# GpSimd's gathers wait for TensorE's counts; masks in the accumulating form with scaled scores; x in fours from tile 8; no dummy products

## What is computed

```
inputs = front_emb[movie_id]                 # 2048 x 64, gathered
true_w, true_b = after_emb[labels], after_bias[labels]
samp_w, samp_b = after_emb[sampled_ids], after_bias[sampled_ids]
true_logits    = sum(inputs * true_w) + true_b - log(expected_count(labels))
sampled_logits = inputs @ samp_w.T + samp_b - log(expected_count(sampled_ids))
sampled_logits = where(sampled_ids == label, sampled_logits - 1e9, sampled_logits)
loss = logsumexp([true_logits, sampled_logits]) - true_logits
```

## Time and profile before

| | before |
|---|---|
| median of 3 runs | 61.03 us (60.61 to 61.16) |
| the profiled execution | 60.93 us |
| its span | 59.0 us |
| GpSimd busy | 40.1 us (68%), 48 instructions |
| VectorE busy | 44.7 us (76%) |
| ScalarE busy | 42.1 us (71%) |
| TensorE busy | 33.5 us (57%) |
| bytes read from HBM | 2.13 MB |

### The profile page before, as it was taken

One profiled execution on the slowest core, in us unless ns is written; L12 is line 12 of the kernel. 1 busy time (PEld: TensorE's weight loads), 2 busy tenths in 40 slices (PEclk: granted clock), 3 DMA queues, 4 the chain that ended last, 5 costly groups with the idle time before them and its releaser, 6 DMA issues.

```text
span 59.0 us, 603 instructions
## 1 busy us (share of the span) xinstructions
PE 33.5 (57%) x137; PEld 22.3 (38%) x137; DVE 44.7 (76%) x129; ACT 42.1 (71%) x69; POOL 40.1 (68%) x48
## 2 busy tenths in 40 slices
PE   0000093998349295997995969696989594000000
PEld 0000044634125254873772556364745481000000
DVE  3799888859688828995897997994999994490830
ACT  5305996489958092999979979999999949209020
POOL 4076777767777777767777776777777677776000
PEclk9999999999999999999999999999999999998555
DMA  0472122212100111100111101010201101101100
GB/s 0 172 192 50 45 62 64 53 45 50 22 22 22 22 42 24 24 22 22 28 25 36 22 22 28 23 23 23 55 24 23 23 23 31 37 23 23 23 0 6
DMA packets 1715, 2.17 MB, mean 37 GB/s; under 512 B 944, under 2 KB 944, under 8 KB 1712
## 3 DMA queue, kind: packets, MB, share of 16 engines
q0 software_dynamic: 1280, 1.59, 11.9%
q1 hardware_dynamic: 432, 0.55, 3.3%
HBM read 2.13 MB, written 0.01 MB: 36 GB/s over the span
## 4 chain that ended last, share of the span: by engine, by line
POOL 63%; issue 21%; DMA 7%; POOLq 2%; DVE 2%; ACT 1%; DVEq 0%
POOL x_rows L221 27%; POOL t_rows L221 23%; POOL w_rows L221 13%; DMA t_rows<-after,rows 4%; DMA id_cols<-ids 3%; POOLq L57 2%; DVE prod L504 0%; ACT rest L371 0%; ACT ratio L369 0%; DVE rows L414 0%; DVE neg_gap L536 0%; DVE wrap L412 0%; DVE loss L539 0%; DVE wrapped L413 0%; DVEq L502 0%
## 5 line engine op out<-in xcount | busy, mean ns | idle before, releaser
L327 ACT ACTIVATE psum<-psum,lowest 128x1024 f32<-128x1024 f32 x16 | 17.2, 1074 | 4.0 <-DVE lowest L494 3.9
L494 DVE CUSTOM_DVE_ANT_0 psum<-psum,masks 128x1024 f32<-128x1024 f32 x16 | 19.5, 1233 | 0.7 <-PE psum L279 0.6
L221 POOL DMA_INDIRECT x_rows<-front,rows x16 | 16.2, 1013 | 4.9 <-issue 4.9
L221 POOL DMA_INDIRECT t_rows<-after,rows x16 | 15.3, 956 | 4.9 <-issue 4.9
L277 PE MATMUL psum<-wT_high,xT 128*128 128x512 f32 x32 | 13.7, 429 | 3.7 <-ACT psum L327 3.7
L279 PE MATMUL psum<-b_parts,ones 128*128 128x512 f32 x32 | 12.7, 396 | 0.0
L278 PE MATMUL psum<-wT_low,xT 128*128 128x512 f32 x32 | 12.6, 395 | 0.0
L308 ACT ACTIVATE masks<-sample_ids,neg_label 128x1024 f32<-128x1024 int32 x8 | 9.2, 1144 | 3.1 <-DMA sample_ids<-sample_row 3.1
L221 POOL DMA_INDIRECT w_rows<-after_twice,rows x8 | 7.7, 965 | 3.8 <-issue 2.1
L313 ACT ACTIVATE masks<-masks,ln_big 128x1024 f32<-128x1024 f32 x8 | 9.2, 1147 | 0.0
L277 PEld LDWEIGHTS psum<-wT_high,xT 128*128 128x128 f32 x32 | 6.0, 188 | 7.3 <-issue 6.5
(11 more groups left out here) (79 smaller groups left out, 30.4 us busy)
## 6 DMA issues: line engine op xcount, KB each, us to landing
sample_ids<-sample_row SPq DMA_DIRECT2D x1, 512.0 KB, 3.9
x_rows<-front,rows POOLq DMA_INDIRECT x16, 2.5
t_rows<-after,rows POOLq DMA_INDIRECT x16, 2.4
w_rows<-after_twice,rows POOLq DMA_INDIRECT x8, 2.5
id_cols<-ids SPq DMA_DIRECT2D x1, 20.0 KB, 1.6
out<-loss SPq DMA_DIRECT2D x1, 8.0 KB, 1.4
```

The lines of the kernel that those rows point to most:

```text
L221: return pool.indirect_dma_start(dst, None, table, bass.IndirectOffsetOnAxis(ap=rows[:, col:col + 1], axis=0))
L327: nc.scalar.activation(logits(t), logits(t), ACT.Exp, bias=lowest[:, t:t + 1], scale=-1.0, accum_out=sums[:, t:t + 1]).then_inc(exp_ok, 1)
L494: V.tensor_tensor_reduce(out=logits(t), in0=logits(t), in1=masks[:, t, :], scale=1.0, scalar=3e38, op0=ALU.add, op1=ALU.min, accum_out=low ...
```

## The change

- **GpSimd.** Twenty-one of the gathers get a wait in front of them, for counts that TensorE gives: transposes of w for w tile 6 and x tile 0, of the bias for x tile 2, of x for x tiles 4 and 5, and finished scores (logits_ok) for later x tiles and for the label tiles. The order of the gathers stays. The count for each tile stands in the two tuples SCORED_BEHIND_X and SCORED_BEHIND_LABELS.
- **Masks.** VectorE's masks are 1 where the ids match, else 0, made by a tensor_scalar that also writes out a sum (accum_out to hits, which nothing reads), from a float copy of the sample ids that ScalarE makes first. ScalarE's masks lose their factor of 1e9. The scores are made smaller by 2 to the power -30 (in the scaling of x and of the bias), and the reduction multiplies by 2 to the power 30 after it has added the mask.
- **x by fours.** Tiles 8 to 11 and 12 to 15 become groups of four: one turn, one raise and one lower each. All places of turning, raising, lowering and masking in the loop are written out anew. Two masks are made ahead of the loop instead of four.
- **Dots.** One over eight tiles behind tile 11, one over four behind tile 15, instead of three over four.
- **No dummy products.**

```diff
--- before.py
+++ after.py
@@ -15,19 +15,24 @@
 BATCH = 2048
 SAMPLE_TILES = SAMPLES // P
 TILES = BATCH // P
-NEG_INF = -1e9
 BANK = 512
 SLOTS = 3
 QUARTERS = 4
 CORR = SAMPLE_TILES + TILES
 
+SHRINK = 2.0 ** -30
+
 SPREAD = P * (CORR + TILES)
 
-X_GROUPS = [(0, 1), (1, 2)] + [(t, t + 2) for t in range(2, TILES, 2)]
+X_GROUPS = [(0, 1), (1, 2), (2, 4), (4, 6), (6, 8), (8, 12), (12, 16)]
 ACT_MASKS = (0, 1, 2, 5, 8, 10, 12, 14)
 
+SCORED_BEHIND_X = (0, 0, 0, 0, 0, 0, 1, 1, 1, 2, 2, 3, 4, 5, 5, 6)
+SCORED_BEHIND_LABELS = (7, 8, 8, 9, 10, 10, 11, 11, 12, 13, 13, 14, 14, 15, 16, 16)
+
 BATCHED = 12
-T_GROUPS = [(0, 4), (4, 8), (8, 12), (12, 13), (13, 14), (14, 15), (15, 16)]
+T_GROUPS = [(0, 8), (8, 12), (12, 13), (13, 14), (14, 15), (15, 16)]
+BATCHES = 2
 
 SQRT_HALF = 0.70710677
 LOG_P = (0.070376836, -0.1151461, 0.116769984)
@@ -74,7 +79,7 @@
         neg_label = sb("neg_label", [P, TILES])
         sample_ids = sb("sample_ids", [P, SAMPLES], i32)
         ident = sb("ident", [P, P])
-        ln_big = sb("ln_big", [P, 1])
+        sample_f = sb("sample_f", [P, SAMPLES])
 
         w_rows = sb("w_rows", [P, SAMPLE_TILES, TWICE + 1])
         x_rows = sb("x_rows", [P, TILES, AUG])
@@ -117,6 +122,7 @@
 
         lowest = sb("lowest", [P, TILES])
         sums = sb("sums", [P, TILES])
+        hits = sb("hits", [P, TILES])
         log_sums = sb("log_sums", [P, TILES])
         base = sb("base", [P, TILES])
         dots = sb("dots", [P, TILES])
@@ -146,7 +152,7 @@
             return slice(a * P, b * P)
 
         def group_of(t):
-            return t if t < 2 else t // 2 + 1
+            return t if t < 2 else t // 2 + 1 if t < 8 else t // 4 + 3
 
         def w_cols(q):
 
@@ -180,6 +186,7 @@
         x_high_ok = sem("x_high_ok")
         xT_ok = sem("xT_ok")
         logits_ok = sem("logits_ok")
+        sample_f_ok = sem("sample_f_ok")
         act_square = sem("act_square")
         act_mask = sem("act_mask")
         dve_mask = sem("dve_mask")
@@ -222,13 +229,26 @@
                                                bass.IndirectOffsetOnAxis(ap=rows[:, col:col + 1], axis=0))
 
             pool.wait_ge(rows_ok, 1)
+
             for j in range(SAMPLE_TILES):
+                if j == 6:
+                    pool.wait_ge(w_turned, 1)
                 gather(w_rows[:, j, :], after_twice, j).then_inc(w_in[j // 2], 16)
             for g in range(len(X_GROUPS)):
                 for t in range(*X_GROUPS[g]):
+                    if t == 0:
+                        pool.wait_ge(w_turned, 2)
+                    elif t == 2:
+                        pool.wait_ge(b_turned, 3)
+                    elif t in (4, 5):
+                        pool.wait_ge(x_turned, t - 3)
+                    elif t >= 6 and SCORED_BEHIND_X[t] > SCORED_BEHIND_X[t - 1]:
+                        pool.wait_ge(logits_ok, SCORED_BEHIND_X[t])
                     gather(x_rows[:, t, 0:EMBED], front, MOV + t).then_inc(x_in[g], 16)
             for k, (a, b) in enumerate(T_GROUPS):
                 for t in range(a, b):
+                    if t == 0 or SCORED_BEHIND_LABELS[t] > SCORED_BEHIND_LABELS[t - 1]:
+                        pool.wait_ge(logits_ok, SCORED_BEHIND_LABELS[t])
                     gather(t_rows[:, t, :], after, LAB + t).then_inc(t_in[k], 16)
 
         @block.tensor
@@ -258,11 +278,6 @@
                     m = nc.tensor.transpose(psum[0:EMBED, x_bank(g), i * P:(i + 1) * P], x_rows[:, t, 0:EMBED],
                                             ident[:, :])
                 m.then_inc(x_turned, 1)
-
-            def keep_busy(n):
-                for _ in range(n):
-                    nc.tensor.matmul(psum[:, 7, :], ones[:, :], ones[:, 0:1].to_broadcast([P, BANK]),
-                                     start=True, stop=True)
 
             def score(t):
                 if t >= SLOTS:
@@ -280,25 +295,22 @@
                 m.then_inc(logits_ok, 1)
 
             turn_w(0)
-            keep_busy(2)
             turn_w(1)
-            keep_busy(4)
             turn_w(2)
             turn_b(0)
             turn_b(1)
             turn_b(2)
-            keep_busy(3)
             turn_w(3)
             turn_x(0)
             turn_b(3)
             turn_x(1)
+
+            turned_behind = {1: 2, 2: 3, 4: 4, 6: 5, 9: 6}
             for t in range(TILES):
-                if t % 2 == 0 and 2 <= t < TILES - 2:
-                    turn_x(group_of(t + 2))
                 pe.wait_ge(xT_ok, group_of(t) + 1)
                 score(t)
-                if t == 0:
-                    turn_x(group_of(2))
+                if t in turned_behind:
+                    turn_x(turned_behind[t])
 
         @block.scalar
         def _(act):
@@ -310,8 +322,7 @@
 
             def hit(t):
                 act.wait_ge(act_square, ACT_MASKS.index(t) + 1)
-                nc.scalar.activation(masks[:, t, :], masks[:, t, :], ACT.Exp, bias=ln_big[:, 0:1],
-                                     scale=-256.0).then_inc(act_mask, 1)
+                nc.scalar.activation(masks[:, t, :], masks[:, t, :], ACT.Exp, scale=-256.0).then_inc(act_mask, 1)
 
             def raise_w(q):
                 act.wait_ge(w_turned, q + 1)
@@ -320,7 +331,7 @@
             def raise_x(g):
                 act.wait_ge(x_turned, g + 1)
                 n = x_cols(g).stop - x_cols(g).start
-                nc.scalar.mul(xT[0:EMBED, x_cols(g)], psum[0:EMBED, x_bank(g), 0:n], -1.0).then_inc(x_high_ok, 1)
+                nc.scalar.mul(xT[0:EMBED, x_cols(g)], psum[0:EMBED, x_bank(g), 0:n], -SHRINK).then_inc(x_high_ok, 1)
 
             def exps(t):
                 act.wait_ge(lowest_ok, t + 1)
@@ -328,6 +339,7 @@
                                      accum_out=sums[:, t:t + 1]).then_inc(exp_ok, 1)
 
             act.wait_ge(row_in, 16)
+            nc.scalar.copy(sample_f[:, :], sample_ids[:, :]).then_inc(sample_f_ok, 1)
             act.wait_ge(labels_ok, 1)
             square(0)
             hit(0)
@@ -343,12 +355,12 @@
             raise_w(2)
             hit(2)
             act.wait_ge(b_turned, 2)
-            nc.scalar.copy(b_parts[0:2, 0:BANK], psum[0:2, 4, :]).then_inc(b_low_ok, 1)
+            nc.scalar.mul(b_parts[0:2, 0:BANK], psum[0:2, 4, :], SHRINK).then_inc(b_low_ok, 1)
             square(5)
             raise_w(3)
             raise_x(0)
             act.wait_ge(b_turned, QUARTERS)
-            nc.scalar.copy(b_parts[0:2, BANK:], psum[0:2, 5, :]).then_inc(b_high_ok, 1)
+            nc.scalar.mul(b_parts[0:2, BANK:], psum[0:2, 5, :], SHRINK).then_inc(b_high_ok, 1)
             raise_x(1)
             hit(5)
             raise_x(2)
@@ -356,10 +368,11 @@
 
             between = {0: (square, 8), 1: (hit, 8), 3: (square, 10), 4: (hit, 10), 6: (square, 12), 7: (hit, 12),
                        9: (square, 14), 10: (hit, 14)}
+            raised_behind = {1: 3, 3: 4, 6: 5, 9: 6}
             for t in range(TILES):
                 exps(t)
-                if t % 2 == 0 and t + 4 < TILES:
-                    raise_x(group_of(t + 4))
+                if t in raised_behind:
+                    raise_x(raised_behind[t])
                 if t in between:
                     make, u = between[t]
                     make(u)
@@ -381,8 +394,8 @@
                 dve.wait_ge(step, linked[0])
 
             def make_mask(t):
-                V.tensor_scalar(masks[:, t, :], sample_ids[:, :], label[:, t:t + 1], -NEG_INF, ALU.is_equal,
-                                ALU.mult).then_inc(dve_mask, 1)
+                V.tensor_scalar(masks[:, t, :], sample_f[:, :], label[:, t:t + 1], None, ALU.is_equal, ALU.add,
+                                accum_out=hits[:, t:t + 1]).then_inc(dve_mask, 1)
 
             def lower_w(q):
                 dve.wait_ge(wT_high_ok, q + 1)
@@ -401,12 +414,11 @@
             def lower_x(g):
                 dve.wait_ge(x_high_ok, g + 1)
                 n = x_cols(g).stop - x_cols(g).start
-                V.scalar_tensor_tensor(xT[EMBED:, x_cols(g)], psum[0:EMBED, x_bank(g), 0:n], -1.0,
+                V.scalar_tensor_tensor(xT[EMBED:, x_cols(g)], psum[0:EMBED, x_bank(g), 0:n], -SHRINK,
                                        xT[0:EMBED, x_cols(g)].bitcast(f32), ALU.mult, ALU.subtract).then_inc(xT_ok, 1)
 
             V.memset(b_parts[:, :].bitcast(f32), 0.0)
             V.memset(ones[:, :].bitcast(f32), 1.0).then_inc(dve_consts_ok, 1)
-            V.memset(ln_big[:, :], math.log(-NEG_INF))
             dve.wait_ge(limits_ok, 1)
             dve.wait_ge(ids_in, 16)
             V.tensor_scalar(wrap[:, :], id_cols[:, :], 0.0, float(VOCAB), ALU.is_lt, ALU.mult)
@@ -470,20 +482,18 @@
             V.tensor_tensor(count[:, :], count[:, :], below[:, :], ALU.add).then_inc(count_ok, 1)
 
 
+            dve.wait_ge(sample_f_ok, 1)
+            make_mask(DVE_MASKS[0])
             lower_w(0)
             lower_w(1)
             dve.wait_ge(log_count_ok, 1)
             split_b(0, 3)
             lower_w(2)
-            dve.wait_ge(row_in, 16)
-            make_mask(DVE_MASKS[0])
```

(30 more changed lines are left out.)

## The result

| | before | changed |
|---|---|---|
| median, side by side on one chip | 61.09 us (60.61 to 61.34, 4 runs) | 64.69 us (64.50 to 65.66, 4 runs) |
| the profiled execution | 60.93 us | 64.5 us |
| its span | 59.0 us | 62.5 us |
| neg_gap starts at | 56.33 | 59.77 |

The changed kernel takes 1.060 times as long (95% interval 1.055 to 1.066). The forecast was 63.6 us. So it is slower, by 3.6 us where 2.6 were forecast. Medians and ranges are over all executions; the ratios leave out those that were more than 1.5% above the fastest one of the same kernel.

What follows compares the result with a forecast made beforehand. GpSimd's gathers bound the kernel before, VectorE a close second. VectorE's chain: 22.0 + 29.5 work + 3.1 waits = 54.6, plus 4.4 tail = 59.0; neg_gap moves +2.7 from 56.33, so 60.93 becomes 63.6 us, range 61.1 to 65.6.

Steps and rivals of the forecast that it cites:

- The bound and the slack: Kernel before: GpSimd's count of gathers sets the end; VectorE's chain of 16 reductions has only some 2 us of slack.
- Masks: VectorE's accumulating masks: 1.25 us each instead of 0.67 start to start, +0.58 per mask, +4.6 us for eight.
- Gathers: GpSimd's x and label gathers: no longer stretched by masks, nearly all 0.94 us, 1.3 us saved by the last gather.
- The clock at the start: TensorE without dummies: score 0 starts at 1.2 GHz; +1.8 us taken, bounds +1.2 (score 0 slow) and +2.4 (both slow).
- The hole at tile 8: Before reduction 8: VectorE waits 1.79 us, as tiles 8 to 11 are lowered as one group behind reduction 7.
- a rival with a chance of 0.12: TensorE's clock falls again between scores 7 and 8; two to three slow scores, 65.5 to 67 us; chance 0.12.
- The sum of the loop: VectorE from reduction 1 to the start of reduction 15: 29.5 us of work plus 3.1 of waits, from 22.0 to 54.6.
- The tail: From the start of reduction 15 to neg_gap: 4.4 us, so neg_gap at 59.0.
- GpSimd's waits: Label tiles 3 and 14 wait for scores 8 and 15; both chains end together; waits by themselves cost 0 to 0.3 us.
- the case of fast masks and slow clock: Rival: 3.5 us less mask work, partly returning as slot waits; neg_gap 56.4 to 57.6, time 61.2 to 62.3; chance 0.12.
- An already met wait I cost at 0: GpSimd's added waits: one whose count has already come costs 0, bounds 0 and 0.1 us each.

Runs made afterwards that it cites:

- b_idle_labels: Kernel before with its 16 label gathers replaced by short memsets to zero: 58.92 us, beside 60.97 for the kernel before.
- a_plain_masks: Changed kernel with VectorE's eight masks back in the plain form, no sum written out: 68.22 us, beside 93.81 for the kernel before.
- after_again: The changed kernel, nothing altered, run again on another chip: 71.21 us, beside 93.70 for the kernel before.
- a_no_waits: Changed kernel with all 21 waits of GpSimd taken out: 99.38 us, beside 93.81 for the kernel before.
- a_group_early: Changed kernel with x tiles 8 to 11 turned, raised and lowered one tile sooner: 66.45 us, 0.712 times the kernel before.
- b_waits: Kernel before with only the 21 waits on GpSimd added: 67.03 us, beside 93.70 for the kernel before.
- b_acc_masks: Kernel before with only the accumulating masks, the scaling and the copy of the ids: 97.08 us, beside 93.70 for the kernel before.
- a_dummies: Changed kernel with the nine dummy products put back: 71.33 us, 0.757 times the kernel before.
- b_fill_labels: Kernel before with label gathers replaced by short memsets, a long memset in front of each: 73.53 us, beside 60.97 for the kernel before.

## Why the prediction was right, point by point

The neg_gap forecast of 59.0 came out at 59.77, and the time of 63.6 at 64.5 for the profiled execution and 64.69 for the median. By its own steps:

- **The bound and the slack.** "VectorE's chain of 16 reductions would end only some 2 us sooner": measured 1.99 us by b_idle_labels. Right, and this is the step on which the sign hung. (Of the gathers beside a mask the forecast says 1.06 to 1.18 us; the trace has 1.02 to 1.19. Its sum of 1.3 us holds.)
- **Masks.** Forecast 1.25 us from start to start, so +0.58 each; measured 1.20 where a reduction follows at once, +0.53. Right. a_plain_masks shows that the form is the cause and that it is worth some 3.0 us, on the second kind of chip.

```profile
28.48 1.27 DVE L397 TENSOR_SCALAR_CACHE_REDUCE masks<-sample_f,label 128x1024 f32<-128x1024 f32 x1
...
29.68 1.23 DVE L504 CUSTOM_DVE_ANT_0 psum<-psum,masks 128x1024 f32<-128x1024 f32 x1
```

- **Gathers.** All at 0.943 us, as forecast. The rule cited there (the Trainium skill, SBUF — State Buffer, Who interferes with whom) has the accumulating form leave GpSimd's port alone; the trace agrees, 943 ns with it and 1013 with the plain form in a_plain_masks.
- **The clock at the start.** The forecast took +1.8 us, midway between score 0 alone slow (+1.2) and scores 0 and 1 (+2.4); only score 0 was. But score 0 started at 17.73 instead of 17.2. The two errors cancel, by luck: reduction 1 starts at 22.09, forecast 22.0. Reduction 0 starts at 20.80, not 20.0. How long the clock stays low isn't the kernel's alone: with the same start it was 6 products here, 9 in after_again and 12 in a_no_waits. And that the missing dummies are the cause isn't shown: no trace without them has a fast score 0, but b_idle_labels has a slow one with them. This term came near to the measured one on an argument that the runs don't bear out.
- **The hole at tile 8.** The place and the mechanism were right, 1.79 us of wait forecast, 3.02 measured. The mis-sized term is the clock: I gave its second fall to a rival with a chance of 0.12 and put 2 to 3 slow scores in it. One score was slow: from its first start to its last end it takes 2.93 us (38.17 to 41.10), where a_group_early, at 2.4 GHz after a shorter wait, needs 1.68 (39.81 to 41.49). The 1.25 us between them are the whole miss of this term. That they are the clock's is shown by the spacing, 0.43 us and not 0.24. The Trainium skill (TensorE: Matmul & The Clock Gate, Part 1) has the low clock as the default state, which activity ends; the forecast drew on that for score 0 and could have for score 8. The trace agrees here, and a_group_early, with 1.31 us of idling instead of 3.2, keeps 2.4 GHz. The length of the last pause doesn't settle it alone: 2.20 us lost the clock in a_plain_masks, 2.55 kept it in b_waits.
- **The sum of the loop.** From reduction 1 to reduction 15 the forecast had 29.5 of work and 3.1 of waits. Measured: 55.34 - 22.09 = 33.25, with waits of 0.43, 3.02, 0.57 and 0.69, together 4.7, so 28.5 of work. The waits are 1.6 more (1.2 of them the clock), the work is 1.0 less: 14 reductions at 1.25 instead of 1.28, masks at 1.20, lowerings 0.3 less together. A dot over eight tiles takes 0.70 + 0.69, forecast 1.4. That the total missed by only 0.8 us is in part luck: too much work and too little wait offset each other, and where the clock stays low for two scores, as in after_again, VectorE waits another 0.77 us, before reduction 10.
- **The tail.** 59.77 - 55.34 = 4.43, forecast 4.4.
- **GpSimd's waits.** Label tile 3 waits for score 8 as forecast (it starts at 41.38, forecast about 40.3), and the last gather starts at 56.83 (forecast 56.15). Tile 14, which the forecast has waiting for score 15, hardly does: 0.34 us in front of it, 0.04 more than usual. Both chains end together, as forecast. The waits were to cost 0 to 0.3 us. In this trace no step of VectorE's loop waits for a gather, and its tail takes 4.43 us, against 4.29 in a_no_waits (89.94 to 94.23), where all labels have long landed: 0.14 us. That is read from two traces; a run without the waits on the first kind of chip is lacking, since a_no_waits landed on the second.
- **A slip in the rivals.** From neg_gap to the end the kernel before has 4.60 us (56.33 to 60.93), so the case of fast masks and slow clock is 61.0 to 62.2 us, not 61.2 to 62.3. It decides nothing.

What the forecast did not see at all is that the price of a wait depends on the chip. On the second kind the same 21 waits turn 94 us into 67, and "An already met wait I cost at 0" isn't even the question there: they are met late, and meeting them makes the pause that lets the counts through. The trace of the kernel before couldn't hint at it, since it was taken on a chip without the delay.

**What stays open.** What differs between the chips. Whether gathers, or any unbroken work of GpSimd, delay TensorE's counts. What makes score 0 slow in one execution and fast in another. And the price of each part on the first kind of chip: it is read from the changed kernel's trace, not from a run. Three estimates of neg_gap there, none of them run: the changed kernel with its group one tile earlier gains at most the wait of 3.02, so 56.75; with plain masks at most 6 x 0.53 = 3.2, so 56.6; neither would beat the 56.33 of the kernel before. For b_acc_masks the gathers would be done 1.3 us sooner, at 55.0, and VectorE's chain, 54.34 in b_idle_labels, gets at most four longer masks in its loop, 2.1 us, so 56.5: it may come out on either side. On the second kind a_group_early (66.45) and b_waits (67.03) are the fastest.

## What to carry to other kernels

Before moving work onto the second-busiest engine, work out its slack against the bound, and hold each new instruction against that number: here 2.0 us of slack met 3.2 us of slower masks and a hole of 3.0. When transfers or lowerings are grouped, look at the first tile of each group: everything on the chain from that one lowering to the next score is exposed, and a pause of TensorE of 2.2 to 3.2 us cost the low clock on top in five traces here, for one score or two (0.2 us for each product of 512 columns), and didn't in one (2.55 us). A time from one chip can hide a stall of another: if an engine shows long waits with no releaser while GpSimd issues gathers without a break, try a pause in them.

## What the runs showed of the hardware that was not expected

- **Late counts.** On three chips, TensorE's counts reached ScalarE, VectorE and GpSimd up to 31 us after its products were done, while GpSimd issued gathers at 1.25 us each. They came through 1.4 to 1.9 us into a pause of GpSimd (b_waits; 2.7 in after_again, at 23.47), or 1.5 us after its last gather (a_no_waits); without a pause a few came singly, after 11.7 and 25.1 us (a_no_waits). Counts of ScalarE to VectorE came at once. In the traces of the first kind of chip the counts were on time throughout.
- **A plain mask against memsets.** A plain tensor_scalar of 128x1024 on VectorE, started inside an unbroken row of memsets on GpSimd, took 14.96 us instead of 0.75 and ended only when the row did. The Trainium skill (SBUF — State Buffer, Who interferes with whom) has the later of the two block until the other's instruction ends; the trace shows the block, but lasting over 28 memsets and not one. A reduction and a lowering of x, just before it, ran beside the same memsets at their usual 1.26 and 0.42 us. Gathers in the same place stretch a mask by far less: the mask at 28.70 beside a gather took 0.75, and the longest plain one beside gathers 0.98 (b_waits, at 22.10). Nothing here tells what in the memsets makes the difference.
- **Accumulating masks.** tensor_scalar with a sum takes 1.28 us for 128x1024, against 0.76 for the plain form on the same data, and its readout 0.08 more that overlaps.
- **The clock falls in a short hole, and not by the hole's length alone.** 3.2 us without work between two scores put TensorE at 1.2 GHz in four traces (the changed kernel's, after_again, a_no_waits, a_dummies), for 6 to 12 products; in a_dummies it fell only at the fourth product behind the hole. 2.20 us did it in a_plain_masks; 1.31 us in a_group_early and 2.55 us in b_waits did not.
- **The same start, two clocks.** With nine dummies ahead of it score 0 ran at 2.4 GHz in the kernel before and in b_fill_labels, and at 1.2 GHz in b_idle_labels, on the same code up to there.
